# One block from QKV to gate/up, with buffers at fixed places and each stage's first inputs prepared in the stage ahead

## The chip, the cores and the metric

The kernel runs on one core of one Trainium2 chip. The metric is the device time of one execution in microseconds (us). TensorE (PE in the profile) multiplies matrices; VectorE (DVE), ScalarE (ACT) and GpSimd (POOL) work element by element; SyncE (SP) issues most of the transfers. Engines run their own streams of instructions in order and wait for one another by semaphores.

## The reference

An AdaLN transformer layer in float32: 2048 tokens, width 1024, 32 query heads and 8 key/value heads of 32 columns, no mask, and a feed-forward part of width 2752 whose activations are truncated to 8-bit integers.

```python
mod = (_silu(L0_c) @ L0_wmod).reshape(L0_c.shape[0], 6, 1, -1)
sa, ca, ga, sb, cb, gb = (mod[:, 0], mod[:, 1], mod[:, 2], mod[:, 3], mod[:, 4], mod[:, 5])
ga = (2 * (ga >= 0) - 1) * jnp.maximum(jnp.abs(ga), 0.25)      # gb likewise
h = _layernorm(x, axis=-1) * (1 + ca) + sa
x = x + ga * _L0_attn_ref(h, L0_attn_Wq, L0_attn_Wk, L0_attn_Wv, L0_attn_Wo, L0_attn_bo)
h = _layernorm(x, axis=-1) * (1 + cb) + sb
x = x + gb * _L0_ffn_ref(h, L0_ffn_w_gate, L0_ffn_w_up, L0_ffn_w_down)
# attention: softmax(q k^T / sqrt(32)) v per head, then y @ Wo.T + bo
# ffn: trunc(clip(silu(xf Wg^T) * (xf Wu^T) * 128)) as int8, @ Wd^T, trunc(clip(* 128))
```

## The kernel before

Five stage functions follow one another, each with its own buffers and its own `nc.Block`. At the end of a block all engines meet at a barrier, and then go to the code of the next block. Float32 operands are split in a high and a low part, and each product is three matmuls (`TERMS`): high by high, high by low, low by high.

- `stage_modulation_and_qkv`: four blocks of 512 tokens. In the last one PE also multiplies the scores for the row maxima of attention's unit 0 (`first_turn`). SP stores the two rows of maxima into `qs0` (line 232). The stage ends when every store of q, k and v has landed (the waits at the end of POOL's and ACT's code).
- `stage_attention`: 32 units, one for each of 8 key/value heads and 4 blocks of 512 queries, with 16 key tiles (k = 0 to 15) each. For a key tile PE makes four transposed score tiles (line 954), ACT takes their exponential (853), and at every even k PE multiplies two earlier key tiles by v (`by_v`, 965). Between them PE multiplies the scores of the next units (`turn`, 940), of which DVE takes maxima (872). POOL adds pairs of exponentials (797), DMAs add such pairs (806), and PE sums three of these over the keys (`denominators`, 980). In unit 0 turns start at k = 2; in unit 31 there are none, and most of unit 30's are done early. After unit 31 PE multiplies the last denominators, DVE takes eight reciprocals (898) and the product (902), SP stores y. The output weights `wo_raw` are loaded early, unsplit.
- `stage_out_projection`: 16 tiles of 128 tokens, in a loop for the middle 12. It first loads y of tiles 0 and 1 (1098), splits y (1147 on ACT, 1177 on DVE) and the weights (1151, 1182), and prepares the gate on DVE (`gate_of`). For tile t PE runs `project(t + 1)`, 48 matmuls (1237), then eight transposes of the normalised tile t (1250); ACT scales them (1165); DVE adds bias, gate and x, and normalises (1207 to 1217), splits y of tile t + 2 and splits the second layer input of tile t - 1 (1198, 1200). All low parts go to memory (`h2lo_dram`) by POOL and come back by SP.
- `stage_gate_up`: 22 tiles of 128 hidden columns, each by four blocks of 512 tokens (n). For each n PE runs 24 matmuls for gate and 24 for up (1446). The next weights are split by ACT (1373) and DVE (1398) within a tile.
- `stage_down`: its own block, before and after the change.

Every engine issues in the order of its code; there is no planner.

Of the kernel before, what the change touches and what calls it, by code (L numbers as in the profile page):

```python
# [11 lines left out]
P = 128  # L12
# [26 lines left out]
def overlay(nc, stack, *views):  # L39

    out = []
    for i, (name, shape, dt) in enumerate(views):
        one = nc.sbuf_tensor(name, shape, dt)
        if i + 1 < len(views):
            with one as tensor:
                out.append(tensor)
        else:
            out.append(stack.enter_context(one))
    return out
# [35 lines left out]
def stage_modulation_and_qkv(nc, ctx, c, wmod, x, wq_t, wk_t, wv_t, mod_dram, q_dram, k_dram, v_dram, modT, ident,  # L85
                             hT0_hi, kq0):
# [14 lines left out]
    with ExitStack() as st:  # L101
        def sb(name, shape, dt=F32):
            return st.enter_context(nc.sbuf_tensor("qkv_" + name, shape, dt))

        def pb(name, width=NB):
            return st.enter_context(nc.psum_tensor("qkv_" + name, [P, width], F32))

        def sem(name):
            return st.enter_context(nc.semaphore("qkv_" + name))

        w = [sb(f"wqkv_{n}", [P, MW, FT, P], F32R) for n in ("hi", "lo")]
        wraws = sb("wqkv_raw", [P, 2, FT, P])
        wraw = [wraws[:, i] for i in range(2)]
        hT_1 = [overlay(nc, st, (f"qkv_wmod_{n}", [P, 2, GW], F32), (f"qkv_hT1_{n}", [P, FT, NB], F32R))
                for n in ("hi", "lo")]
        hT = [[hT0_hi, sb("hT0_lo", [P, FT, NB], F32R)], [i[1] for i in hT_1]]
        xt = [sb(f"x_tile{i}", [P, D]) for i in range(2)]
        stats = [sb(f"ln_stats{i}", [P, 12]) for i in range(2)]
        mv = [sb(f"ln_mv{i}", [P, 2]) for i in range(2)]
        s = [sb(f"ln_s{i}", [P, 8]) for i in range(2)]  # L120
        aff = [sb(f"h_affine{i}", [P, FT, P]) for i in range(2)]
        qko = [[sb(f"qk_out{i}_{n}", [P, NB], F32R) for n in ("hi", "lo")] for i in range(2)]
        vo = [sb(f"v_out{i}", [P, VW]) for i in range(2)]
        ccol, cwork = sb("c_col", [P, FT]), sb("c_work", [P, 3, FT])
        ones, crep = sb("ones_32", [P, 32]), sb("silu_c_rep", [P, FT, 32])
        rows = sb("mod_rows", [P, NB])
        wmod_own = sb("wmod", [P, GW])
# [6 lines left out]
        cmax0, rmax0 = sb("chunk_max0", [P, NTURN]), sb("row_max0", [P, GH * BT])  # L134
        mT0 = [sb(f"max_T0_{n}", [GH * BT, P], F32R) for n in ("hi", "lo")]
        tr = pb("h_T", 2 * NB)
        qkp = [pb(f"qk_acc{i}") for i in range(QKB)]
        vp = [pb(f"v_acc{i}") for i in range(2)]
        modp = pb("mod_acc")

# [28 lines left out]
        block = st.enter_context(nc.Block(no_gpsimd_drain=True))  # L169
# [25 lines left out]
        def _(sp):  # L195
# [77 lines left out]
        def _(act):  # L273
# [50 lines left out]
            for i in range(2):  # L324
                act.wait_ge(v_stored[i], 16 * TT // 2)

# [215 lines left out]


def stage_attention(nc, ctx, q_dram, k_dram, v_dram, y_dram, den_dram, kq0, ident, wo_t, wo_raw, wo_loaded):
# [35 lines left out]
    with ExitStack() as st:  # L580
        def sb(name, shape, dt=F32):
            return st.enter_context(nc.sbuf_tensor("att_" + name, shape, dt))
# [50 lines left out]
        def bank(u, c, i):  # L633

            return (order(u, c) + i) % NST
# [1186 lines left out]
```

## Time and profile before

| | us |
|---|---|
| median of three runs | 3582.47 (3580.29 to 3582.48) |
| the profiled execution | 3583.01 |
| its span, first to last instruction | 3581.2 |
| PE busy | 3462.8 (97%) |
| DVE busy | 2218.3 (62%) |
| POOL busy | 1602.9 (45%) |
| ACT busy | 1600.1 (45%) |

The span is what the trace covers; the execution's own time is 1.8 us longer. The stages hold about these stretches of the span: QKV 0 to 375, attention 383.6 to 2052, output projection 2055 to 2262, gate/up 2271 to 3238, down 3241 to 3581. "PEclk" in a row of the windows view is the TensorE clock that was granted: 1.00 is 2.4 GHz, 0.50 is 1.2 GHz.

### The profile page before, as it was taken

The numbers are of one execution on the slowest core, as the hardware profiler recorded it, in microseconds if no ns is written. First come the engines' busy times: TensorE is split into PE (matmuls) and PEld (weight loads), VectorE is DVE, ScalarE is ACT, GpSimd is POOL, SyncE is SP. The second block draws the span as 40 slices with busy tenths as digits, with TensorE's granted clock in tenths as the row PEclk, the third lists the DMA queues.
The fourth block names the chain that finished last, engine by engine and source line by source line (L and its number), as shares of the span: only waits on it lengthen the run. The fifth ranks groups of instructions, "written<-read, shape, count | busy, mean of one in ns | idle before, by whom it ended". The sixth has DMA issues, their size and how long they took to land. (4 is left out here: it accounts for less than half of the span.)

```text
span 3581.2 us, 46156 instructions
## 1 busy us (share of the span) xinstructions
PE 3462.8 (97%) x17196; PEld 2314.1 (65%) x17196; DVE 2218.3 (62%) x3730; ACT 1600.1 (45%) x2990; POOL 1602.9 (45%) x701
## 2 busy tenths in 40 slices
PE   6999899999999999999999699799999999998998
PEld 4778455555555555555555288688888888887786
DVE  5545677777777777777777088444444444442727
ACT  3210466666666666666666433222222222213544
POOL 1111488989989899899889700000000000000010
PEclk8999899999999999999999899899999999999999
DMA  6662555656555555556554445611111111113212
GB/s 228 206 189 82 131 119 107 123 109 123 112 115 113 112 121 111 116 112 122 110 107 95 91 166 173 182 29 29 29 30 29 29 29 29 30 41 118 94 64 86
DMA packets 196090, 361.96 MB, mean 101 GB/s; under 512 B 41744, under 2 KB 122896, under 8 KB 175696
## 3 DMA queue, kind: packets, MB, share of 16 engines
q0 software_dynamic: 37120, 202.92, 24.9%
q1 hardware_dynamic: 156496, 154.69, 15.7%
q8 instruction: 104, 1.70, 0.2%
q10 hardware_dynamic: 2304, 2.10, 0.2%
q14 instruction: 66, 0.54, 0.0%
HBM read 162.13 MB, written 62.78 MB: 63 GB/s over the span
## 5 line engine op out<-in xcount | busy, mean ns | idle before, releaser
L872 DVE TENSOR_REDUCE att_chunk_max<-att_scores 128x1 f32<-128x512 f32 x1984 | 1212.9, 682 | 352.1 <-PE att_scores L940 352.1
L853 ACT ACTIVATE att_exp<-att_scores_T 128x512 f32<-128x512 f32 x2048 | 1049.5, 621 | 449.9 <-PE att_scores_T L954 441.8
L797 POOL TENSOR_TENSOR att_exp_pair<-att_exp 128x2048 f32<-128x2048 f32 x256 | 1199.7, 4737 | 62.8 <-ACT att_exp L853 62.3
L965 PE MATMUL att_y_acc<-att_exp,att_v_head 128*32 128x512 f32 x4096 | 499.0, 605 | 0.0
L1327 POOL DMA_DIRECT2D inter_scratch<-gu_inter x84 | 45.2, 538 | 882.6 <-DVE gu_inter L1270 882.6
L940 PE MATMUL att_scores<-att_kq,att_q_stack 96*128 96x512 f32 x768 | 327.3, 430 | 3.8 <-DMA att_q_stack<-q_scratch 2.4
L940 PE MATMUL att_scores<-att_k_stack,att_q_stack 96*128 96x512 f32 x768 | 325.0, 426 | 0.3
L954 PE MATMUL att_scores_T<-att_q_stack,att_k_stack 98*128 98x512 f32 x768 | 299.3, 412 | 2.4 <-ACT att_exp L853 2.3
L954 PE MATMUL att_scores_T<-att_q_stack,att_kq 98*128 98x512 f32 x768 | 296.4, 405 | 0.7 <-ACT att_exp L853 0.7
L1381 ACT ACTIVATE gu_magnitude<-gu_value 128x512 f32<-128x512 f32 x88 | 55.7, 633 | 516.7 <-DVE gu_value L1412 516.7
L1411 DVE TENSOR_TENSOR gu_rounded<-gu_up_acc,gu_rounded 128x512 f32<-128x512 f32 x88 | 60.9, 692 | 323.7 <-PE gu_up_acc L1446 323.7
L965 PEld LDWEIGHTS att_y_acc<-att_exp,att_v_head 128*32 128x32 f32 x4096 | 107.4, 109 | 216.6 <-ACT att_exp L853 116.7
L940 PEld LDWEIGHTS att_scores<-att_kq,att_q_stack 96*128 96x128 f32 x768 | 144.8, 189 | 149.3 <-DVE att_chunk_max L872 86.8
L1446 PE MATMUL gu_gate_acc<-h_hi,shared_split 128*128 128x512 f32 x704 | 225.7, 392 | 11.7 <-DVE shared_split L1398 11.7
L940 PEld LDWEIGHTS att_scores<-att_k_stack,att_q_stack 96*128 96x128 f32 x768 | 144.3, 188 | 139.4 <-DVE att_chunk_max L872 77.2
L1446 PE MATMUL gu_up_acc<-h_hi,shared_split 128*128 128x512 f32 x704 | 223.9, 389 | 0.0
L954 PEld LDWEIGHTS att_scores_T<-att_q_stack,att_k_stack 98*128 98x128 f32 x768 | 144.3, 189 | 74.5 <-ACT att_exp L853 49.6
L954 PEld LDWEIGHTS att_scores_T<-att_q_stack,att_kq 98*128 98x128 f32 x768 | 145.1, 189 | 55.5 <-ACT att_exp L853 32.6
L1237 PE MATMUL wo_wo_acc<-wo_wo_hi,shared_split 128*128 128x512 f32 x512 | 164.2, 397 | 13.7 <-DVE shared_split L1177 13.5
L806 POOL DMA_DIRECT2D att_exp_pair<-att_exp_pair x128 | 111.7, 873 | 127.5 <-DMA att_exp_pair<-att_exp_pair 93.2
L1446 PEld LDWEIGHTS gu_gate_acc<-h_hi,shared_split 128*128 128x128 f32 x704 | 133.2, 189 | 40.0 <-issue 12.1
L1446 PEld LDWEIGHTS gu_up_acc<-h_hi,shared_split 128*128 128x128 f32 x704 | 132.2, 188 | 27.5
(222 smaller groups left out, 6059.8 us busy)
## 6 DMA issues: line engine op xcount, KB each, us to landing
att_exp_pair<-att_exp_pair POOLq DMA_DIRECT2D x128, 1024.0 KB, 7.2
att_q_stack<-q_scratch SPq DMA_DIRECT2D x72, 256.0 KB, 5.8
shared_raw<-in_wd_t POOLq DMA_DIRECT2D x34, 256.0 KB, 3.3
qkv_x_tile<-in_x SPq DMA_DIRECT2D x16, 512.0 KB, 4.7
q_scratch<-qkv_qk_out_hi POOLq DMA_DIRECT2D x32, 256.0 KB, 3.1
q_scratch<-qkv_qk_out_lo POOLq DMA_DIRECT2D x32, 256.0 KB, 4.2
qkv_wqkv_raw<-in_wmod POOLq DMA_DIRECT2D x8, 1024.0 KB, 7.3
qkv_wmod<-in_wmod POOLq DMA_DIRECT2D x8, 1024.0 KB, 8.2
```

The source lines that it names most:

```text
L797: nc.gpsimd.tensor_tensor(ps[PAIR_SLOT[j]][:], pr[2 * j % NP][:], pr[(2 * j + 1) % NP][:], ALU.add).then_inc(pair_done, 1)
L806: pool.dma_start(ps[into][:], ps[other][:], accum_op=ALU.add).then_inc(dma_sum[i], 16)
L853: nc.scalar.activation(pr[k % NP][:, h * NB:(h + 1) * NB], stp[bank(u, c, GH * k + h)][:], ACT.Exp, scale=INV_SQRT_DH).then_inc(exp_done, 1)
L872: nc.vector.reduce_max(cmax[c % 2][:, q:q + 1], turn_buffer(u, c, q)[:], AX.X).then_inc(sm_done, steps_done(u, q))
L940: nc.tensor.matmul(turn_buffer(u, c, q)[:], qs[c % 4][0:SR, h, qt * P:(qt + 1) * P], ks[c // QB % 2][0:SR, kc * NB:(kc + 1) * NB], start=T ...
L954: nc.tensor.matmul(stp[bank(u, c, i)][:], ks[c // QB % 2][0:SR + 2, k * P:(k + 1) * P], qs[c % 4][0:SR + 2, h, :], start=True, stop=True). ...
L965: ins = nc.tensor.matmul(yp[h * DH:(h + 1) * DH, :], vg[c // QB % 2][:, k, :], pr[k % NP][:, h * NB:(h + 1) * NB], start=(k == 0), stop=(k ...
L1237: ins = nc.tensor.matmul(acc[j][:, half * NB:(half + 1) * NB], ysp[j][a][:, k, :], w[z][:, k, half * NB:(half + 1) * NB], start=(k == 0 an ...
L1327: eng.dma_start(inter_dram[i, 0:LASTI if last else P, n * NB:(n + 1) * NB], out[n % 2][rows, :]).then_inc(last_stored if last else out_sto ...
L1381: nc.scalar.activation(mag[:], val[:], ACT.Abs)
L1411: ln.link(nc.vector.tensor_tensor(rnd[:], up[n % 2][:], rnd[:], ALU.mult))
L1446: ins = nc.tensor.matmul(bank[n % 2][:], w[j][a][:, m * HALF_W + k * P:m * HALF_W + (k + 1) * P], h2[z], start=(k == 0 and q == 0), stop=( ...
```

## The change

QKV, attention, output projection and gate/up share one `nc.Block`. The three barriers between them are gone, and semaphores that the stages hand on take their place. All buffers get fixed offsets (`place`, `bank`), so that what one stage fills does not lie on what the one ahead still uses.

- QKV to attention: SP loads q of units 1 and 2 and v of the first head within QKV, ahead of its wait for unit 0's maxima; ACT runs one Exp at the end of QKV. PE's attention code waits for `v_evac` at its start and for `qk_evac` at k = 2.
- Attention: the output weights are loaded in unit 0 as 16 transfers. Their high parts are copied by ACT in units 30 and 31 (eight copies of 128x512 each, two after h = 2 of k = 2, 4, 8, 10), their low parts by DVE after unit 30's work, with the reciprocal of unit 30 in between. y of tiles 0 and 1 is loaded and split within unit 31. The last denominators, division and store of y go into the output projection's tiles 0 and 1.
- Output projection: unrolled, no loop. The gate and bias loads go from POOL's queue to SP's, after unit 31's scores. Low parts of tiles 0 to 3 stay on chip (`h2_lo0`). The first gate/up weights are loaded at t = 14 and split by ACT and DVE around t = 14 and 15. The last tile's transposes, scaling, split and store of x go into gate/up's first tile.
- Gate/up: tiles 0 and 1 are taken out of the loop. For n = 0 the low part is read as four pieces of 128 columns, because `h2_lo0` is laid out by tile.
- Down keeps its block, now `nc.Block()` without `no_gpsimd_drain`.

```diff
@@ stage_modulation_and_qkv, SP: ahead of the wait for mT0_done
+            for u in (1, 2):
+                for r, n in enumerate((0, 0, 1)):
+                    sp.dma_start(qs[u][r * DH:(r + 1) * DH].bitcast(F32),
+                                 q_dram[n].rearrange("(h d) t -> d h t", d=DH)[:, 0:GH, u * NB:(u + 1) * NB].bitcast(F32)
+                                 ).then_inc(q_loaded[u], 16)
+            for i in range(2):
+                sp.wait_ge(v_stored[i], 16 * TT // 2)
+            sp.dma_start(vg[0][:], v_dram[:, 0:DH].rearrange("(k p) d -> p k d", p=P)).then_inc(v_loaded, 16)
...
@@ stage_attention, SP
+                if u == NU - 1:
+                    sp.wait_ge(y_stored, 16 + 16 * (NU - 2))
+                    sp.wait_ge(*first_y_room)
+                    sp.wait_ge(pv_done, NP + u * KT + KT // 2 + 2)
+                    for t in range(2):
+                        wo.load_y(sp, t)
...
@@ stage_attention, ACT
+                        if u >= NU - 2 and k in WO_HI_AT and h == GH - 2:
+                            for i in (2 * WO_HI_AT.index(k), 2 * WO_HI_AT.index(k) + 1):
+                                act.wait_ge(wo.loaded, 32 * FT)
+                                nc.scalar.copy(wo.hi[:, u - NU + 2, i, :], wo.raw[:, u - NU + 2, i, :]).then_inc(wo.hi_done, 1)
+                        if u == NU - 1 and k == TSTEP and h == GH - 2:
+                            act.wait_ge(*first_y_room)
+                            act.wait_ge(pv_done, NP + u * KT + KT // 2 + 2)
+                            wo.hi_of_y(act, 0)
...
@@ stage_attention, DVE
-            units(v, unit)
-            last_unit(NU - 1, NU - 1)
+            for u in range(NU - 1):
+                unit(u, u % BODY, u // QB)
+            wo_lo(0, range(FT))
+            wo_lo(1, range(FT // 2))
+            recip(NU - 2)
+            wo_lo(1, range(FT // 2, FT))
+            for t in range(2):
+                wo.lo_of_y(v, t)
...
@@ stage_out_projection, ACT
+            for t in range(TT):
+                if t == TT - 1:
+                    act.wait_ge(acc_done, TT)
+                    gu.weights_hi(act, 0, 0, 1)
                 act.wait_ge(var_done, t + 1)
...
+                if t == TT - 2:
+                    act.wait_ge(acc_done, TT - 1)
+                    act.wait_ge(gu.loaded[0], 32)
+                    gu.weights_hi(act, 0, 0, 0)
+                if t < TT - 1:
+                    affine(act, t)
...
@@ stage_out_projection, DVE: ahead of tile 15, and after tile 0
+                if t == TT - 1:
+                    for m in range(2):
+                        gu.weights_lo(v, 0, 0, m)
...
+                if t == 0:
+                    att["division"](v)
+                else:
+                    split(v, t - 1)
...
@@ stage_out_projection, PE
+            project(0)
+            for t in range(TT - 1):
+                if t:
+                    pe.wait_ge(x1_done, t)
+                project(t + 1)
+                if t == 0:
+                    att["denominators"](pe)
+                transposes(pe, t)
...
@@ stage_gate_up, PE
+                    pe.wait_ge(out_proj["h_split"], BT * (n + 1))
+                    if n:
+                        pe.wait_ge(h_loaded[n], 16 * BT)
...
+                            low = h2_lo[n][:, k, :] if n else h2_lo0[:, :, k, :]
...
+                    if is_first(i) and n == 0:
+                        out_proj["transposes"](pe)
...
@@ build
+        with nc.Block(no_gpsimd_drain=True) as block:
+            qkv = stage_modulation_and_qkv(nc, ctx, block, c, wmod, x, wq_t, wk_t, wv_t, mod_dram, q_dram, k_dram, v_dram,
+                                           modT, ident, kq0, qs, vg, q_loaded, v_loaded)
...
+        with nc.Block() as block:
+            stage_down(nc, ctx, block, wd_t, mod_dram, x1_dram, inter_dram, out, shared[0], down_loaded)
```

New functions that it calls are `OutInputs` (`load_y`, `hi_of_y`, `lo_of_y`: one transfer, one ACT copy and one DVE subtraction for a tile of y) and `GateUpWeights` (`weights_hi`, `weights_lo`: the same for one half of a tile's weights).

## Rows read from the trace of the kernel before

**Rows 1.** The page, busy time of each engine and its share of the span.
```profile
PE 3462.8 (97%) x17196; PEld 2314.1 (65%) x17196; DVE 2218.3 (62%) x3730; ACT 1600.1 (45%) x2990; POOL 1602.9 (45%) x701
```
**Rows 2.** Windows: length, busy us (instructions) of each engine, PEclk, DMA share, GB/s.
```profile
385.00:390.00 5.00, 3.26 (x7) 1.73 (x6) 0.00 (x0) 3.90 (x8) 1.51 (x1) 0.50 0.98 200
...
1985.00:2029.00 44.00, 42.37 (x190) 13.71 (x189) 0.26 (x1) 27.92 (x56) 39.37 (x13) 0.89 0.50 103
```
**Rows 3.** Timeline of PE, QKV to attention: start, length, work [idle before <-releaser].
```profile
383.55 4.71 PE L954 MATMUL att_scores_T<-att_kq 98*128 98x512 f32 x9 [8.65 <-DVE att_ones L921]
390.62 1.22 PE L940 MATMUL att_scores<-att_kq,att_q_stack 96*128 96x512 f32 x2 [2.36 <-DMA att_q_stack<-q_scratch]
...
393.90 3.64 PE L965 MATMUL att_y_acc<-att_exp,att_v_head 128*32 128x512 f32 x16
...
404.18 1.92 PE L965 MATMUL att_y_acc<-att_exp,att_v_head 128*32 128x512 f32 x16
```
**Rows 4.** Timeline of SP's queue, the store of unit 0's maxima.
```profile
373.74 0.57 SPq L232 DMA_DIRECT2D att_kq<-qkv_max_T_lo  x1
```
**Rows 5.** Line 232, time of its two transfers from issue to landing.
```profile
DMA to landing us min/median/max: 2.4/2.6/2.8
```
**Rows 6.** Timeline of PE, attention to output projection.
```profile
2030.14 1.90 PE L980 MATMUL att_den_acc<-att_exp_pair,att_ones 128*32 128x512 f32 x16
2045.91 1.94 PE L980 MATMUL att_den_acc<-att_exp_pair,att_ones 128*32 128x512 f32 x8 [13.87 <-DMA att_exp_pair<-att_exp_pair]
2061.33 0.79 PE L1237 MATMUL wo_wo_acc<-wo_wo_hi,shared_split 128*128 128x512 f32 x1 [13.48 <-DVE shared_split L1177]
```
**Rows 7.** Timeline of ACT in unit 31.
```profile
2014.17 4.03 ACT L853 ACTIVATE att_exp<-att_scores_T 128x512 f32<-128x512 f32 x8 [1.39 <-PE att_scores_T L954]
```
**Rows 8.** Timeline of POOL, its last adds.
```profile
2029.63 8.97 POOL L797 TENSOR_TENSOR att_exp_pair<-att_exp 128x2048 f32<-128x2048 f32 x2
```
**Rows 9.** Line 797, ns min/median/max, 500 to 1900 us.
```profile
L797 POOL TENSOR_TENSOR att_exp_pair<-att_exp x221: 4555/4862/4922, 499.8 to 1899.1; 128x2048 f32<-128x2048 f32 x111
```
**Rows 10.** Line 797, ns min/median/max, 1975 to 2040 us.
```profile
L797 POOL TENSOR_TENSOR att_exp_pair<-att_exp x10: 4493/4710/4882, 1979.2 to 2034.1; 128x2048 f32<-128x2048 f32 x10
```
**Rows 11.** Timeline of DVE, last division and first tile of the output projection.
```profile
2047.91 3.45 DVE L898 RECIPROCAL att_den_acc<-att_den_acc 128x64 f32<-128x64 f32 x8 [39.97 <-PE att_den_acc L980]
2051.40 0.69 DVE L902 TENSOR_TENSOR att_y_out<-att_y_raw,att_den_acc 128x512 f32<-128x512 f32 x1
...
2075.84 1.23 DVE L1207 TENSOR_TENSOR wo_gated<-wo_wo_acc,wo_bo_rows 128x1024 f32<-128x1024 f32 x1 [0.90 <-PE wo_wo_acc L1237]
...
2082.90 0.81 DVE L1217 TENSOR_SCALAR wo_x_norm<-wo_x_tile,wo_ln_mv,wo_ln_s 128x1024 f32<-128x1024 f32 x1
2083.63 1.22 DVE L1177 TENSOR_TENSOR shared_split<-shared_raw,shared_split 128x1024 fp32r<-128x1024 f32 x1
```
**Rows 12.** Timeline of PE, last tiles of the output projection to gate/up.
```profile
2239.71 1.04 PE L1250 MATMUL wo_h_T<-ident,wo_x_norm 128*128 128x128 f32 x8
2240.51 0.47 PE L1237 MATMUL wo_wo_acc<-wo_wo_hi,shared_split 128*128 128x512 f32 x1
...
2251.52 1.03 PE L1250 MATMUL wo_h_T<-ident,wo_x_norm 128*128 128x128 f32 x8
2259.64 1.97 PE L1250 MATMUL wo_h_T<-ident,wo_x_norm 128*128 128x128 f32 x8 [7.09 <-DVE wo_x_norm L1217]
2273.33 0.77 PE L1446 MATMUL gu_gate_acc<-h_hi,shared_split 128*128 128x512 f32 x1 [11.72 <-DVE shared_split L1398]
```
**Rows 13.** Timeline of ACT at the same place.
```profile
2252.59 2.89 ACT L1165 ACTIVATE wo_h_affine<-wo_h_T,mod_cols 128x128 f32<-128x128 f32 x8 [6.70 <-PE wo_h_T L1250]
...
2270.78 1.99 ACT L1373 CAST shared_split<-shared_raw 128x1024 fp32r<-128x1024 f32 x2 [6.08 <-PEq L1040]
```
**Rows 14.** Timeline of PE, gate/up's second block of tokens, its second matmul.
```profile
2286.91 0.39 PE L1446 MATMUL gu_gate_acc<-gu_h_lo,shared_split 128*128 128x512 f32 x1
```
**Rows 15.** Windows, line 505 alone: length, busy us (matmuls), then busy us (weight loads).
```profile
115.10:125.00 9.90, 9.90 (x83) 9.90 (x83) 1.00 0.84 270
```

More of the change, by code:

```diff
@@ L36, with place, bank, in_order @@
 SHARED = max(6 * HALF_W, IT * QW)
[L39 to L48, printed above, removed]
+R0 = 704
+R1, R2, R3, R4, R5, BIG = (R0 + n * 1024 for n in (16, 32, 40, 48, 56, 64))
+TAIL = BIG + 140 * 1024
+PR, PS = BIG, BIG + 64 * 1024
+WO_AT, DEN_AT_ROW = BIG + 104 * 1024, BIG + 136 * 1024
+def place(nc, offset, name, shape, dt):
+    if offset == 0:
+        with nc.sbuf_tensor(name, shape, dt) as tensor:
+            return tensor
+    with nc.sbuf_tensor("below_" + name, [P, offset // 4], F32):
+        with nc.sbuf_tensor(name, shape, dt) as tensor:
+            return tensor
+def bank(nc, nth, name, width=NB):
+    if nth == 0:
+        with nc.psum_tensor(name, [P, width], F32) as tensor:
+            return tensor
+    with nc.psum_tensor("below_" + name, [P, nth * NB], F32):
+        with nc.psum_tensor(name, [P, width], F32) as tensor:
+            return tensor
+def in_order(first, *sizes):
+    out = [first]
+    for n in sizes:
+        out.append(out[-1] + n)
     return out
@@ L914, in unit @@
                             recip(u - 1)
-                    if not ahead and k == RECIP_AT:
-                        recip(u - 1)
                     if k == TSTEP - 2 and not beyond(u, 1):
@@ L1068, in stage_out_projection @@
-        y_hi, y_split, acc_done, x1_done, x1_stored = (
-            sem("y_hi"), sem("y_split"), sem("acc_done"), sem("x1_done"), sem("x1_stored"))
+            return ctx.enter_context(nc.semaphore("wo_" + name))
+        BT = NB // P
+        xt = [sb(f"x1_tile{i}", [P, D], F32, R2 + i * 4 * D) for i in range(2)]
+        gate, bias = sb("gate_a", [P, D], F32, R3), sb("bo_rows", [P, D], F32, R3 + 4 * D)
+        offs = in_order(BIG + 4 * SHARED, 4 * D, 4 * D, 4 * D, 4 * D)
+        work, xn, aff = sb("gated", [P, D], F32, offs[0]), sb("x1_norm", [P, D], F32, offs[1]), sb("h2_affine", [P, FT, P], F32, offs[2])
@@ new lines, in affine, with split @@
+        def affine(act, t):
+            act.wait_ge(tr_done, t + 1)
+            act.wait_ge(h_split, t)
+            for f in range(FT):
+                ins = nc.scalar.activation(aff[:, f, :], tr[f * P // NB][:, f * P % NB:f * P % NB + P], ACT.Identity,
+                                           scale=modT[:, 32 + f:33 + f], bias=modT[:, 24 + f:25 + f])
+            ins.then_inc(aff_done, 1)
+        def split(v, t):
+            v.wait_ge(aff_done, t + 1)
+            if t == BT - 1:
+                v.wait_ge(*att["y_stored"])
+            if t > BT:
+                v.wait_ge(lo_stored, 16 * (t - BT))
+            for half in range(2):
+                fs = slice(half * FT // 2, (half + 1) * FT // 2)
+                hi = h2_hi[half][:, :, t * P:(t + 1) * P]
+                low = h2_lo0[:, t, fs] if t < BT else lo[t % 2][:, fs]
+                nc.vector.tensor_copy(hi, aff[:, fs]).then_inc(h_hi, 1)
+                v.wait_ge(h_hi, t * 2 + (half + 1))
+                ins = nc.vector.tensor_tensor(low, aff[:, fs], hi.bitcast(F32), ALU.subtract)
+            ins.then_inc(h_split, 1)
@@ L1128, in _ @@
[L1128 to L1129 removed]
+                    load_x(t + 2)
+                if t == 1:
+                    att["store_y"](sp)
+                    sp.wait_ge(*att["y_stored"])
         @block.gpsimd
         def _(pool):
[L1133 to L1135 removed]
@@ L1307, in stage_gate_up @@
+        h_loaded = [None] + [sem(f"h2lo_loaded{b}") for b in range(1, QB)]
         g_acc, u_acc, sig_done, val_done, parts_done, out_done, out_stored = (
```

637 lines of the change are left out of this document (311 added, 326 removed).

## The prediction

> **What bounds the kernel now.** I read the page's busy shares first. PE is busy 97% of the span and the next engine 62% [rows 1], so time can be gained only where PE stands still or runs at its lower clock. The chain of waits gives nothing on the change: it follows PE back through the down stage alone. I therefore went through PE's timeline at each change of stage, then through the other engines' timelines at the same places.
>
> From QKV to attention PE stands still 8.65 us, then 2.36 us for unit 1's q [rows 3]. From attention to the projection it stands still 13.87 us for the last sum by DMA and 13.48 us for the first y [rows 6]. From the projection to gate/up it stands still 7.09 and 11.72 us [rows 12]. That is 57.2 us in six gaps. After a gap PE also runs at the 1.2 GHz level: the clock is 0.50 in the window after the first [rows 2], and `by_v` takes 3.64 us there against 1.92 later [rows 3]. The gap at down is outside this change.
>
> **A: QKV to attention.** The last QKV matmul ends at 374.9 (383.55 - 8.65) [rows 3]. What unit 0 still needs is its row of maxima: issued at 373.74 [rows 4], landed 2.4 to 2.8 us later [rows 5], so about 376.4; with some 0.4 us for SP to pass its semaphores on, PE starts at 376.8 in place of 383.55. That gives 6.75 us. Of the new waits at PE's start, `v_evac` belongs to values multiplied 60 us earlier, and behind it stands all of attention, so only the maxima count. The wait for `qk_evac` at k = 2 has PE's turns and `by_v` behind it; k = 2 comes about 4.7 us after the start (the length of the first run of scores [rows 3]), when DVE has long split the last tile. DVE's fill of a constant (under 2 us) fits before that as well. The 2.36 us for q go too, since those six loads and that of v are issued some 50 us earlier. On SP they stand behind unit 0's own q and k, so they delay no first turn; the wait for v's stores stands ahead of SP's wait for the maxima, and v is finished by then. A = 9.1 us.
>
> What is late next is ACT: during k = 0 and 1 PE goes at the pace of the exponentials and may again run at the lower clock. The row of that stretch has PE busy 3.26 of 5 us at 0.50 [rows 2], but a long gap stands before it. In unit 31 there are only short waits for ACT, and the clock still averages 0.89 over 44 us [rows 2]. I take the low clock at first, so nothing more is gained on the first `by_v`. The other end is 3.64 - 1.92 = 1.7 us more [rows 3]. The 16 weight loads on SP (8 before) stand ahead of unit 1's maxima store, which is due a whole unit later; no cost.
>
> The Trainium skill ("TensorE: Matmul & The Clock Gate", Loop structure matters more than you think) says that waiting for a copy out of PSUM does not break PE's warmth, only a long wait for a DMA does. By it the new start would stay at 2.4 GHz and A would be 10.8 us. The unit 31 row speaks against it, so it does not change my term.
>
> **B: attention to projection.** `by_v` of unit 31 ends at 2030.1, where the denominators start now [rows 6]. PE goes straight to `project(0)`. ACT has two copies more at each of four places in unit 31, 0.5 to 0.6 us each (half of a copy of 1024 columns, 1.0 us, and a little for the start) [rows 13], about 1.2 us together. They stand just where ACT waits 1.39 us for PE after h = 2 [rows 7], so they hide; in unit 30, where the turns lengthen each pair of key tiles, the wait is longer. If that cover were gone, PE would lose up to 16 x 0.6 = 9.6 us over both units. y of tile 0 is loaded after POOL's fifth pair of unit 31, about 2016 (two adds and two smaller jobs ahead of 2029.6 [rows 8]), and is copied (1.0 us) [rows 13] in the same kind of hole at k = 14.
>
> `project` is 11.0 us (2240.51 to 2251.52) and eight transposes 0.8 us (2239.71 to 2240.51) [rows 12]. Before, `project(0)` ended at about 2075.8, when DVE took it up [rows 11]; new it ends at 2030.1 + 11.0 = 2041.1: 34.7 us earlier. `project(1)` ends at 2052.1. There the denominators come: 1.90 us for two thirds [rows 6], so 2.9 us, to 2055.0. Their last input comes now at 2045.9 [rows 6], so it is not waited for. DVE then takes the reciprocals and product, 3.45 + 0.69 [rows 11], to 2059.2, and only then tile 1, whose chain to the normalised tile is 7.9 us (2075.84 to 2083.7) [rows 11]: 2067.1, plus 1.2 us for y of tile 3 (line 1177) [rows 11], 2068.3. PE would be ready for the transposes of tile 1 at 2066.8 and for `project(3)` at 2067.6, so it loses about 0.8 us. DVE's load a tile stays just under PE's 11.8, so the loss is not repeated. The store of y and its landing hold SP until about 2070; y of tile 4 is needed about 2078. The gate and bias loads, moved to SP, are needed by 2041 and are issued about 2030; if they land at 2039, `gate_of` ends 2.5 us late, and DVE still reaches the division before the denominators. B = 34.7 - 2.9 - 0.8 = 31.0 us. Without the 2.9 us as new work this is the two gaps, the 3.8 us of denominators and 3.7 us of low clock in the first tile.
>
> One cost has no row. DVE now does 16 subtractions with both inputs on chip, and two of y, while POOL adds pairs almost without pause. Before, DVE's work beside POOL was maxima from PSUM. If neither disturbs the other, the cost is zero: POOL's add has a median of 4.86 us beside a busy DVE and 4.71 with DVE idle [rows 9, 10], so reading PSUM costs it little. At the other end each excludes the other for an instruction: DVE gets about one subtraction in between two adds of 4.7 us, so 12 of them take until about 2020 (they start at 1974), the reciprocal of unit 30 and thus SP's load of y follow, and the split of y comes after POOL's last add. That add ends at 2038.6 now [rows 8] and some 4 us later with DVE's pieces between, so `project(0)` starts at about 2043: 13 us. I take 2 us, near the zero that these rows favour.
>
> The Trainium skill ("SBUF — State Buffer", Who interferes with whom) says that a DVE instruction with two SBUF inputs and a GpSimd instruction that reads SBUF lock each other out. No row of before has that pair, so it can't be checked; by the rule the sum loses 11 us of the 58 below. It is a rival.
>
> **C: projection to gate/up.** Let E be 2251.52, when the transposes of tile 14 start [rows 12]. Before, the second block of tokens starts one matmul (0.23) ahead of 2286.91 [rows 14]: E + 35.2. New: transposes to E + 0.8, gate's 24 matmuls (half a `project`, 5.5) to E + 6.3. Up needs its weights: ACT scales tile 14 until E + 4.0 [rows 13], copies for 1.0 us [rows 13], DVE subtracts for 1.2 (1024 columns, as for y) [rows 11]: E + 6.2, just in time. Up ends at E + 11.8. DVE starts tile 15 at E + 6.2 (before: E + 0.2) and has it normalised at E + 14.1, so PE waits 2.3 us, transposes, and starts the second block at E + 15.0. C = 35.2 - 15.0 = 20.2 us. Gate's own weights are loaded from E - 14 on and split at E - 2; ACT's wait for that load has the scaling of tile 14 behind it. If they came 8 us late, C would lose 6. Sigmoid comes with its table load after the last square root, and the last tile's split is due only at the fourth block, at about E + 37; these hide. The low parts loaded back are three blocks instead of four. The peeled tiles issue the same work.
>
> The pieces of 128 columns in gate/up's n = 0 are 22 x 16 = 352 matmuls. Line 505 already reads its moving operand in two such pieces: 83 matmuls of 256 columns in 9.90 us, 0.119 each [rows 15], the same for a column as 0.23 for 512. I cost them at zero; the upper bound is double their 0.227, 80 us. Fixed places alone change no instruction: zero, and a stage of 1650 us bounds it by no row, so I allow 2 us either way. Down's `nc.Block()` may add under 1 us at the end, where POOL is idle.
>
> **The sum.** 9.1 + 31.0 - 2 + 20.2 = 58.3 us. From the profiled execution's 3583.0 that is 3524.7; the median lies 0.5 us below that execution: 3524.
>
> **Rivals.**
> - Ports: DVE and POOL shut each other out in unit 31. For: they do overlap. Against: nothing in these rows shows it. Loss 13 in place of 2: 3535.
> - The barrier's waits live on: one start still waits for a store, a load or a copy. The likeliest is A (maxima landing and the lower clock both later, giving 2 us) or C's weights late (6 us less): 3531. The change then does only part of what it says. Against: each of these inputs has its landing in the rows above.
> - Slower: the 128-column pieces halve PE's rate in those 352 matmuls, 80 us: 3604. It decides from 58.3 / 352 = 0.166 us each. Against: line 505's pace.
> - Better: clock kept, no cost at ports: 3524 - 1.7 - 2 = 3520, inside the forecast.
>
> **Chances.** Forecast 0.55, ports 0.24, waits that live on 0.14, pieces 0.04, and 0.03 for a loss without a name that eats the gain. The range goes from 3514 (6 us past the better case, as copies or clock may give more) to 3541 (ports and late weights together). 0.2%, 7 us, is about what a measurement can tell here: faster by more 0.94, within 0.02, slower 0.04.
>
> **What would show it.** Right: PE gaps of about 2 us at the first place, under 2 at the second, about 2.3 before the last transposes; the first out-projection matmul at about 2023 (2030.1 - 9.1 + 2); denominators after `project(1)`. Wrong in B: DVE's subtractions in unit 31 with starts tied to the ends of POOL's adds, or waits of ACT longer than its copies. Wrong in A: the first score after 377. Wrong at the pieces: starts of those matmuls more than 0.23 us apart. A sum of gaps gone below 45 us would make the prediction wrong.

## The result: 3555.0 us, half of the gain that was forecast

| | before | changed |
|---|---|---|
| median, us | 3581.85 | 3555.02 |
| lowest to highest, 4 runs each | 3580.29 to 3582.48 | 3551.06 to 3556.60 |
| ratio, 95% interval | | 0.9924 [0.9907, 0.9941] |
| profiled execution, us (its span) | 3583.0 (3581.2) | 3555.3 (3553.4) |

The change makes the kernel 26.8 us faster. The forecast was 58 us, to 3524, with a range of 3514 to 3541; the measured time lies outside it.

**Where the gain came.** Read at fixed points of PE's timeline: the first denominators of the attention start 3.8 us earlier (the two rows below, before and after). The transposes of tile 14 start 21.7 us earlier [rows 12], and gate/up's second token block 27.4 us earlier [rows 14]. From there to the end nothing changed. So A gave 3.8 us (forecast 9.1), B 17.9 (29.0) and C 5.7 (20.2). These are readings of one execution each. In the traces of experiments 1, 4, 5, 6 and 7, whose code is the same up to the first denominators, these start at 445.3 to 448.5, so A is 2.5 to 5.7 us.

```profile
450.99 1.04 PE L980 MATMUL att_den_acc<-att_exp_pair,att_ones 128*32 128x512 f32 x8
```
```profile
447.21 1.04 PE L744 MATMUL att_den_acc<-att_exp_pair,att_ones 128*32 128x512 f32 x8
```

The page after, against [rows 1]. DVE is busy 56 us longer with eight instructions more:

```profile
PE 3458.6 (97%) x17196; PEld 2311.9 (65%) x17196; DVE 2274.3 (64%) x3738; ACT 1589.2 (45%) x2990; POOL 1604.0 (45%) x695
```

**QKV to attention**, PE's timeline, then ACT's, then POOL's (start, length, engine, line, work, [idle before <-releaser]); against [rows 3]:

```profile
375.72 0.97 PE L1034 MATMUL att_scores_T<-att_kq 98*128 98x512 f32 x3 [1.55 <-SPq L806]
384.50 3.32 PE L1034 MATMUL att_scores_T<-att_kq 98*128 98x512 f32 x6 [7.81 <-ACT att_exp L922]
...
390.73 3.08 PE L1045 MATMUL att_y_acc<-att_exp,att_v_head 128*32 128x512 f32 x16
```
```profile
383.85 4.60 ACT L922 ACTIVATE att_exp<-att_scores_T 128x512 f32<-128x512 f32 x9 [64.01 <-POOLq L898]
```
```profile
376.45 0.54 POOL L283 DMA_DIRECT2D q_scratch<-qkv_qk_out_lo  x1
```

PE's scores start at 375.7, even ahead of the forecast 376.8. Then PE stops after three of them, for 7.81 us, because ACT makes no exponential. The releaser of ACT is not an engine's work but line 898 in POOL's queue: `sem_inc(pair_done, NP // 2)`, the starting value that says "the eight exponential buffers are free". It needs nothing, but it stands in POOL's queue behind the end of POOL's QKV code, a wait for the last stores of q and k. The last of them was issued at 376.45, and the transfers of that line from 372 to 378 took up to 7.0 us to land:

```profile
DMA to landing us min/median/max: 3.2/4.5/7.0
```

**Attention to projection**, DVE's timeline, then ACT's and PE's; against [rows 6, 11]:

```profile
1970.06 45.19 DVE L977 TENSOR_TENSOR wo_lo<-wo_raw,wo_hi 128x512 fp32r<-128x512 f32 x12
2015.17 0.24 DVE L972 RECIPROCAL att_rden_spread<-att_den_spread 128x16 f32<-128x16 f32 x1
2015.33 16.59 DVE L977 TENSOR_TENSOR wo_lo<-wo_raw,wo_hi 128x512 fp32r<-128x512 f32 x4
```
```profile
2027.66 1.04 ACT L1129 CAST shared_split<-shared_raw 128x1024 fp32r<-128x1024 f32 x1 [6.27 <-DMA shared_raw<-y_scratch]
```
```profile
2029.25 1.28 PE L1034 MATMUL att_scores_T<-att_q_stack,att_k_stack 98*128 98x512 f32 x2 [6.04 <-ACT att_exp L922]
2030.47 3.64 PE L1045 MATMUL att_y_acc<-att_exp,att_v_head 128*32 128x512 f32 x16
2037.42 0.80 PE L1314 MATMUL wo_acc<-wo_hi,shared_split 128*128 128x512 f32 x1 [3.32 <-DVE shared_split L1133]
```

The two gaps of 13.9 and 13.5 us are gone, two smaller ones came. DVE's 16 subtractions last 61.8 us. The line's summary gives least, median and most in ns:

```profile
L977 DVE TENSOR_TENSOR wo_lo<-wo_raw,wo_hi x16: 678/4891/10383, 1970.1 to 2026.9; 128x512 fp32r<-128x512 f32 x16
```

The median is one addition of POOL (4.86 us [rows 9]) and the longest is two of them back to back. One subtraction of DVE and the addition of POOL beside it:

```profile
1976.45 5.06 DVE L977 TENSOR_TENSOR wo_lo<-wo_raw,wo_hi 128x512 fp32r<-128x512 f32 x1
```
```profile
1975.94 5.03 POOL L866 TENSOR_TENSOR att_exp_pair<-att_exp 128x2048 f32<-128x2048 f32 x1
```

It ends at 1981.51, 0.54 us after the addition (1980.97), and every long subtraction of this trace ends so, 0.54 to 0.56 us after one of POOL's instructions. The reciprocal of unit 30 stands behind 12 subtractions, SP's load of y behind the reciprocal, and ACT's copy of y stands in front of the last five exponentials. So PE loses 6.04 us inside the attention and 3.32 us after it. How the loss divides changes from one execution to the next: in experiment 2, with the same code here, PE stops once for 16.14 us inside the attention and not after it, but the time from the first denominators to the projection's first matmul is nearly the same, 1591.8 us there and 1590.2 here.

**Projection to gate/up**, PE's timeline, then DVE's and ACT's; against [rows 12, 13]:

```profile
2229.86 1.04 PE L1196 MATMUL wo_h_T<-ident,wo_x_norm 128*128 128x128 f32 x8
2245.26 0.76 PE L1536 MATMUL gu_gate_acc<-h_hi,shared_split 128*128 128x512 f32 x1 [14.36 <-issue]
...
2259.55 0.40 PE L1536 MATMUL gu_gate_acc<-gu_h_lo,shared_split 128*128 128x512 f32 x1
```
```profile
2245.13 0.69 DVE L1219 TENSOR_TENSOR wo_h_lo<-wo_h_affine,h_hi 128x512 fp32r<-128x512 f32 x1
```
```profile
2245.24 1.28 ACT L1468 ACT_TABLE_LOAD   x1 [3.43 <-DVEq L1513]
```

PE stands still 14.36 us and the profile names only "issue": no semaphore event of a compute instruction or a transfer explains it. ACT's row at the same moment names the cause. Line 1513 in DVE's queue is `v.sem_inc(val_done, 2)`, again a starting value. It stands behind all of DVE's projection code, whose last instruction started at 2245.13.

### The profile page after: what moved, and what is told of

Read it like the earlier page. It is cut to its first block and busy times, and to the rows that moved or that the text cites. A ratio compares the mean times of both kernels' runs of the same rounds, so it can differ in the third digit from the quotient of the medians.

```text
span 3553.4 us, 45601 instructions
## 1 busy us (share of the span) xinstructions
PE 3458.6 (97%) x17196; PEld 2311.9 (65%) x17196; DVE 2274.3 (64%) x3738; ACT 1589.2 (45%) x2990; POOL 1604.0 (45%) x695
## 5 line engine op out<-in xcount | busy, mean ns | idle before, releaser
L1314 PE MATMUL wo_acc<-wo_hi,shared_split 128*128 128x512 f32 x512 | 163.2, 396 | 3.4 <-DVE shared_split L1133 3.3
L1536 PEld LDWEIGHTS gu_gate_acc<-h_hi,shared_split 128*128 128x128 f32 x704 | 133.3, 189 | 42.4 <-issue 14.6
L1468 ACT ACTIVATE gu_sigmoid<-gu_gate_acc 128x512 f32<-128x512 f32 x88 | 52.7, 599 | 235.5 <-PE gu_gate_acc L1536 235.5
```

Source lines behind the costliest of these rows:

```text
L1314: ins = nc.tensor.matmul(acc[t % 2][:, half * NB:(half + 1) * NB], wo.ysp[t % 2][a][:, k, :], (wo.hi, wo.lo)[z][:, half, k, :], start=(k = ...
L1536: ins = nc.tensor.matmul(dst, gu.w[j][m][a][:, k * P:(k + 1) * P], h2[z], start=(k == 0 and q == 0), stop=(k == FT - 1 and q == 2))
```

## Experiments

Times below are medians; each ratio is to the kernel before, run on the same chip. The intervals are about 6 us to either side, so a smaller difference from the changed kernel rests on its trace and not on the ratio. Unless a diff says otherwise all else is as in the changed kernel.

### 1. No wait for gate/up's starting value

```diff
                 for n in range(QB):
-                    pe.wait_ge(val_done, n + 1 + i * QB)
+                    if not (is_first(i) and n < 2):
+                        pe.wait_ge(val_done, n + 1 + i * QB)
...
-                    act.wait_ge(val_done, n + 2 + i * QB)
+                    if not (is_first(i) and n == 0):
+                        act.wait_ge(val_done, n + 2 + i * QB)
```

> Edit: TensorE does not wait on the value counter for the first two token blocks of gate/up tile 0, nor ScalarE for the first; the counter's starting value is given by VectorE from its gate/up code, which stands behind its whole output projection. Theory (credit): in the changed kernel TensorE stands 14.4 us ahead of its first gate matmul (to 2245.3) for that starting value alone. Without the wait the gate's 24 matmuls start within 2 us of tile 14's transposes (2229.9), the granted clock stays at full speed there, and tile 15's transposes and the second token block follow VectorE's last normalisation, at about 2244 to 2247 where it was 2259.2: 3555 becomes 3541 to 3544. Rival (the gap is TensorE's own: loading of instructions, or the weights' split): the gap stays above 10 us and the time stays at 3553 to 3556.

Measured: 3540.7 us (3538.6 to 3542.5), ratio 0.9889 [0.9872, 0.9906]. PE's timeline:

```profile
2227.68 1.04 PE L1196 MATMUL wo_h_T<-ident,wo_x_norm 128*128 128x128 f32 x8
2228.47 0.47 PE L1538 MATMUL gu_gate_acc<-h_hi,shared_split 128*128 128x512 f32 x1
...
2241.57 1.09 PE L1196 MATMUL wo_h_T<-ident,wo_x_norm 128*128 128x128 f32 x8 [1.91 <-DVE wo_x_norm L1295]
...
2242.73 0.39 PE L1538 MATMUL gu_gate_acc<-gu_h_lo,shared_split 128*128 128x512 f32 x1
```

The gap is gone, 14.3 us with it. The second block starts 0.23 us ahead of 2242.73, 14.8 us after tile 14's transposes; the forecast's working had 15.0, and 1.9 us of wait where it had 2.3. The instruction stream and the weights hold nothing up.

### 2. No wait for the exponentials' starting value

```diff
-                            act.wait_ge(pair_done, k // 2 + 1 + u * PAIRS)
+                            if not (is_first(u) and k < NP):
+                                act.wait_ge(pair_done, k // 2 + 1 + u * PAIRS)
```

> Edit: ScalarE does not wait on GpSimd's pair counter for the first 8 key blocks of the first unit (their exponential buffers are free; the counter's starting value is given by GpSimd behind its wait for the last stores of QKV). Theory (credit through GpSimd): the first exponential starts at 377 to 378 where it was 383.9, so the first product with V is at 384 to 385 instead of 390.7, and the time is 5 to 7 us lower, 3548 to 3550. Rival (the exponentials or the scores are held by SP's loads or by the table load as well): the first product with V stays after 388, and the time changes by less than 3 us.

Measured: 3547.2 us (3546.0 to 3548.5), ratio 0.9907 [0.9890, 0.9923], 7.8 us less than the changed kernel, slightly more than expected. ACT's timeline, then PE's:

```profile
376.63 4.51 ACT L923 ACTIVATE att_exp<-att_scores_T 128x512 f32<-128x512 f32 x9 [56.17 <-PE att_scores_T L1035]
```
```profile
377.28 3.01 PE L1035 MATMUL att_scores_T<-att_kq 98*128 98x512 f32 x6 [0.22 <-ACT att_exp L923]
...
383.17 2.13 PE L1046 MATMUL att_y_acc<-att_exp,att_v_head 128*32 128x512 f32 x16
```

The first denominators start at 438.69, 12.3 us earlier than before. That is 3.2 us more than A's 9.1; experiment 8 has the same code here and gives 10.0, because its first score came at 378.33 where this one's came at 376.10. From the first score to the first denominators both take 62.6 us, against 67.4 before: 4.8 us less, where the forecast counted only the 2.36 us for unit 1's q. The clock is part of it. Windows of 378 to 392 us (length, busy us of PE, PEld, DVE, ACT and POOL, granted clock, DMA share, GB/s), the changed kernel and then this one:

```profile
378.00:392.00 14.00, 7.50 (x21) 4.27 (x25) 3.26 (x6) 5.79 (x11) 4.02 (x1) 0.55 1.01 343
```
```profile
378.00:392.00 14.00, 13.43 (x52) 6.59 (x55) 9.78 (x18) 8.78 (x17) 6.66 (x2) 0.88 0.99 337
```

With only short waits for ACT the clock averages 0.88 and the first `by_v` takes 2.13 us; behind the 7.8 us gap it is 0.55 and 3.08 us. The Trainium skill ("TensorE: Matmul & The Clock Gate", Loop structure matters more than you think), whose rule on copies out of PSUM the forecast set aside for unit 31's row, comes closer here: its A was 10.8 us, and 2.13 us is nearer to `by_v` at full clock (1.92 [rows 3]) than to the 3.64 that the forecast took.

### 3. Wo's loads a unit later

```diff
-                if is_first(u):
+                if u == 1:
                     for half in range(2):
                         for k in range(FT):
                             sp.dma_start(wo.raw[:, half, k, :], ...)
```

> Edit: the 16 loads of Wo are issued in unit 1 of the attention instead of unit 0; the waits stay as they are. It tells how much of the late start of the exponentials is the landing of the last stores of QKV behind those loads. Theory (crowding): the stores land in about 3.3 us as in the kernel before (issued at 376.4, so at 379.7), and the first exponential starts at 380 where it was 383.9: 3551 to 3552. Rival (the stores are late for another cause, such as the three loads of q in unit 0): the first exponential stays at 383 to 384 and the time at 3555.

Measured: 3563.0 us (3555.1 to 3566.5), ratio 0.9946 [0.9929, 0.9962]: 8 us slower than the changed kernel in the median, but one of the four runs, 3555.1, was not slower at all. At the place that was asked about, the first exponential came at 382.65, neither 380 nor 384. The landing of the stores (line 255 before, then line 283 here):

```profile
DMA to landing us min/median/max: 2.7/3.0/3.3
```
```profile
DMA to landing us min/median/max: 2.7/3.9/5.4
```

Its longest is 5.4 us, where the changed kernel had 7.0. That doesn't show that the sixteen loads are part of the crowding: in experiment 1, where they stand in unit 0 as in the changed kernel, the longest is 5.2 us and the first exponential comes at 382.75. Why the stores land later than before (3.3) stays open. The loss came in unit 1. SP's timeline, then PE's:

```profile
443.16 13.49 SPq L821 DMA_DIRECT2D wo_raw<-in_wo_t  x16
...
466.67 7.38 SPq L792 DMA_DIRECT2D den_scratch<-att_den_rows  x1
```
```profile
482.50 0.80 PE L1020 MATMUL att_scores<-att_kq,att_q_stack 96*128 96x512 f32 x1 [7.23 <-DVE att_chunk_max L952]
```

One issue in SP's queue after those loads lasted 7.38 us; no other of that line takes over 0.6 us in this trace. The loads are the only edit, but why this one issue took so long is not shown. Unit 0's denominators come late by it. DVE waits for them with its reciprocal (7.3 us), the maxima queued behind it are not taken, and PE stops for 7.23 us. In unit 0 the same loads cost nothing of the kind, since no trip of denominators follows them there.

### 4. Wo's low parts in 4 instructions instead of 16

```diff
-                for k in ks:
-                    v.wait_ge(wo.hi_done, half * FT + k + 1)
-                    nc.vector.tensor_tensor(wo.lo[:, half, k, :], ...).then_inc(wo.lo_done, 1)
+                for k in ks[::4]:
+                    v.wait_ge(wo.hi_done, half * FT + k + 4)
+                    nc.vector.tensor_tensor(wo.lo[:, half, k:k + 4, :], ...).then_inc(wo.lo_done, 4)
```

> Edit: the 16 subtractions of 512 columns that make Wo's low parts are 4 of 2048 columns. Theory (VectorE and GpSimd exclude each other, and a subtraction gets in only between two additions of GpSimd): each of the 4 lasts one wait for an addition, up to 4.9 us, and its own 2.4 us, so 4 last under 30 us in place of 61; the reciprocal of unit 30's denominators runs before 2008 instead of 2015.2, ScalarE no longer holds the last exponentials for y (6.3 us), and the output projection starts at 2028 to 2032 instead of 2037.4: 3546 to 3550. Rival (a shared rate: both engines slow down in proportion to what they move): 4 of 2048 columns last as long as 16 of 512, about 15 us each, the last reciprocal is at 2015 or later, and the time is 3554 to 3557.

Measured: 3545.0 us (3543.3 to 3546.1), ratio 0.9899 [0.9882, 0.9915], 10.0 us less. DVE's timeline, then POOL's and PE's:

```profile
1970.20 9.63 DVE L977 TENSOR_TENSOR wo_lo<-wo_raw,wo_hi 128x2048 fp32r<-128x2048 f32 x2
1989.67 11.56 DVE L977 TENSOR_TENSOR wo_lo<-wo_raw,wo_hi 128x2048 fp32r<-128x2048 f32 x1 [9.84 <-ACT wo_hi L931]
2001.36 0.25 DVE L972 RECIPROCAL att_rden_spread<-att_den_spread 128x16 f32<-128x16 f32 x1
2010.52 2.29 DVE L977 TENSOR_TENSOR wo_lo<-wo_raw,wo_hi 128x2048 fp32r<-128x2048 f32 x1 [8.90 <-ACT wo_hi L931]
```
```profile
2011.04 6.19 POOL L866 TENSOR_TENSOR att_exp_pair<-att_exp 128x2048 f32<-128x2048 f32 x1
```
```profile
2026.55 0.50 PE L1314 MATMUL wo_acc<-wo_hi,shared_split 128*128 128x512 f32 x1
```

The same columns take 23.5 us in 4 instructions and 61.8 in 16. The last one, which starts before POOL's next addition, lasts 2.29 us, and the addition that starts inside it lasts 6.19 us instead of 4.86. The exclusion works both ways. The projection starts 10.9 us earlier than in the changed kernel and somewhat ahead of what was expected.

### 5. The same work in 32 instructions

```diff
-                    nc.vector.tensor_tensor(wo.lo[:, half, k, :], ...).then_inc(wo.lo_done, 1)
+                    for cs in (slice(0, NB // 2), slice(NB // 2, NB)):
+                        ins = nc.vector.tensor_tensor(wo.lo[:, half, k, cs], ...)
+                    ins.then_inc(wo.lo_done, 1)
```

> Edit: the 16 subtractions of 512 columns are 32 of 256, the same work in twice the instructions. Theory (VectorE gets in between two additions of GpSimd, one or so instruction each time, whatever its size): their mean stays near 3.8 us each while GpSimd adds, so only some 14 to 17 of 32 are done when its last addition ends at about 2036, the reciprocal (behind 24 of them) runs at 2036 or later, y is late, and the output projection starts at 2050 or later: 3566 or more. Rival (a shared rate): 32 of half the size last half as long each, 1.9 us, nothing moves: 3553 to 3557.

Measured: 3558.5 us (3558.2 to 3558.9), ratio 0.9936 [0.9919, 0.9952], 3.5 us more than the changed kernel, which the intervals don't tell apart; the expectation of 3566 or more missed, and so, by little, did the rival's 3553 to 3557. DVE's windows (length, busy us and instructions of `wo_lo`, clock, DMA) and POOL's timeline:

```profile
2008.00:2012.00 4.00, 4.00 (x1) 1.00 1.04 211
2012.00:2016.00 4.00, 4.00 (x12) 1.00 0.42 84
```
```profile
2007.36 4.86 POOL L866 TENSOR_TENSOR att_exp_pair<-att_exp 128x2048 f32<-128x2048 f32 x1
2014.25 0.87 POOL L875 DMA_DIRECT2D att_exp_pair<-att_exp_pair  x1 [2.03 <-DMA att_exp_pair<-att_exp_pair]
```

While POOL adds, one instruction of half the size is as stuck as one of full size. When POOL waits 2.03 us for a transfer, DVE does about a dozen in 4 us. About half of these run beside POOL's next addition, from 2014.86, and this time it is the addition that is held: it lasts 6.74 us. "One for each addition" left out POOL's pauses. The reciprocal, behind 24 of the 32, came at 2017.1. A rate shared between the engines, the rival, gives neither row of DVE.

### 6. The reciprocal behind 8 subtractions instead of 12

```diff
-            wo_lo(1, range(FT // 2))
             recip(NU - 2)
-            wo_lo(1, range(FT // 2, FT))
+            wo_lo(1, range(FT))
```

> Edit: in the last unit VectorE takes the reciprocal of unit 30's denominators after 8 of the 16 subtractions instead of after 12; sizes unchanged. It separates the two costs of the slow subtractions. Theory (both count): the reciprocal runs at 2005 to 2008 instead of 2015.2, ScalarE no longer waits 6.3 us for y, TensorE ends the attention at about 2027 to 2028 instead of 2034.1, but Wo's and y's low parts are still subtracted one for each of GpSimd's additions and end near 2033 to 2036, so the output projection starts there (2037.4 before): 3550 to 3554. Rival (only the late reciprocal counts): the output projection starts by 2029, and the time is 3545 to 3547.

Measured: 3555.8 us (3547.8 to 3560.1), ratio 0.9921 [0.9904, 0.9937]: no gain, and a wide spread. In the profiled execution, the longest of the four:

```profile
1971.98 43.48 DVE L977 TENSOR_TENSOR wo_lo<-wo_raw,wo_hi 128x512 fp32r<-128x512 f32 x8
```

The reciprocal follows at 2015.38, where it was at 2015.17 in the changed kernel. Eight took as long as twelve had, because in the changed kernel the ninth to the twelfth had cost almost nothing. They ran in one pause of POOL between two additions:

```profile
2012.76 2.49 DVE L977 TENSOR_TENSOR wo_lo<-wo_raw,wo_hi 128x512 fp32r<-128x512 f32 x4
```

So the edit could bring the reciprocal at most 2.5 us forward, and here the eight also started 1.9 us later. A subtraction's cost depends on where POOL stands, and a count of them is no measure of time. The experiment was meant to separate the late reciprocal from the late low parts, and it does not.

### 7. Short additions on POOL in the last unit

```diff
-                nc.gpsimd.tensor_tensor(ps[PAIR_SLOT[j]][:], ...)
+                cs = slice(0, GH * NB // 4 if u == NU - 1 else GH * NB)
+                nc.gpsimd.tensor_tensor(ps[PAIR_SLOT[j]][:, cs], ...)
...
-                nc.gpsimd.tensor_tensor(ps[4][:], ps[4][:], ps[1][:], ALU.add).then_inc(quad_done, 1)
+                cs = slice(0, GH * NB // 4 if u == NU - 1 else GH * NB)
+                nc.gpsimd.tensor_tensor(ps[4][:, cs], ps[4][:, cs], ps[1][:, cs], ALU.add).then_inc(quad_done, 1)
```

> Left out: in the last unit GpSimd's eight pair sums and its sum of four add only the first 512 of their 2048 columns, so the last block's denominators are not whole; its waits and its DMA sums are unchanged, and so are all of VectorE's 16 subtractions of 512 columns. Theory (VectorE's slow subtractions wait for GpSimd's additions): with additions of 1.2 us in place of 4.8 the 16 subtractions last 0.7 to 1.9 us each, under 30 us in all (61.8 in the changed kernel), the ninth to the sixteenth end soon after ScalarE's last high parts (2010), the reciprocal of unit 30 runs by 2007, and the output projection starts at 2026 to 2028: 3543 to 3546. Rival (they are slow from the DMA traffic or from ScalarE's reads of the same buffers, both unchanged): they stay at a median near 4.9 us, and the output projection starts at 2035 or later.

Measured: 3537.6 us (2 runs), ratio 0.9875 [0.9846, 0.9903]. DVE's work on `wo_lo` is unedited:

```profile
L979 DVE TENSOR_TENSOR wo_lo<-wo_raw,wo_hi x16: 676/684/5061, 1969.6 to 2006.3; 128x512 fp32r<-128x512 f32 x16
```
```profile
2021.01 0.50 PE L1316 MATMUL wo_acc<-wo_hi,shared_split 128*128 128x512 f32 x1
```

The median falls from 4.89 to 0.68 us. The long ones left stand beside unit 30's whole additions, but for one of 3.83 us beside two short ones back to back. POOL's additions are the cause. The projection also starts 5 us earlier than expected, and the clock is part of it. Windows of 2000 to 2015 us, the changed kernel, this one, and experiment 1, whose additions are whole:

```profile
2000.00:2015.00 15.00, 14.56 (x54) 4.38 (x54) 15.00 (x7) 10.96 (x23) 12.64 (x6) 0.77 0.54 109
```
```profile
2000.00:2015.00 15.00, 14.34 (x64) 5.08 (x56) 2.76 (x5) 12.81 (x27) 7.09 (x7) 1.00 0.98 210
```
```profile
2000.00:2015.00 15.00, 14.34 (x70) 5.10 (x70) 15.00 (x9) 12.80 (x26) 12.66 (x5) 1.00 0.49 98
```

PE is busy about as long in all three and gets fewer matmuls done at 0.77. The traces of experiments 4 and 8 have the dip too (0.77), those of 5 and 6 don't (1.00). Experiment 1 has the changed kernel's code up to here and stays at 1.00, so the shorter additions are not shown to have removed the dip; its cause stays open. In the changed kernel it seems to cost nothing: experiment 1, without it, takes as long from the first denominators to the projection (1590.5 us against 1590.2), since it waits longer for y.

### 8. The three edits together

Edits 1, 2 and 4.

> Edit: the changed kernel with the three edits together: no wait for the two starting values (first exponentials; first gate/up blocks) and Wo's low parts in 4 instructions. Theory (three separate hidden waits are all that is missing): the gains add, 14.3 + 7.8 + 10.0 = 32.1 us off the changed kernel's 3555.0: 3521 to 3525, and the sum on record (3524) is met. Rival (they share a part, or what is late next takes some of it back): 3527 or more; the place to look is VectorE's wait for the rows of bo ahead of the output projection's first tile, which appeared when the projection started earlier.

Measured: 3523.8 us (3522.8 to 3525.2), ratio 0.9839 [0.9823, 0.9855]. The gains add, and this is the fastest version: 31 us under the changed kernel. PE's timeline at the fixed points:

```profile
440.97 1.04 PE L744 MATMUL att_den_acc<-att_exp_pair,att_ones 128*32 128x512 f32 x8
...
2020.56 0.50 PE L1315 MATMUL wo_acc<-wo_hi,shared_split 128*128 128x512 f32 x1
...
2213.17 1.04 PE L1197 MATMUL wo_h_T<-ident,wo_x_norm 128*128 128x128 f32 x8
...
2228.22 0.39 PE L1539 MATMUL gu_gate_acc<-gu_h_lo,shared_split 128*128 128x512 f32 x1
```

A is 10.0 us (450.99 - 440.97), A and B together 38.4 (2251.52 - 2213.17 [rows 12]), so B 28.3, and C 20.3 (2286.91 - 2228.22 = 58.7, less 38.4) [rows 14]. The recorded terms were 9.1, 29.0 and 20.2. DVE's wait of 8.9 us for the rows of bo, named by the rival, is there, and PE loses 1.3 us to it at the first transposes. PE also waits 1.5 us for the last sum by DMA, which the forecast expected to be early.

## Why the prediction was wrong

**The sum is that of a kernel without three waits; the changed kernel has them.** Each of the three takes back what its experiment returned: 14.3 + 7.8 + 10.0 = 32.1 us, and 3555.0 less that is 3522.9. What is left after them came to within 1 us of each term in experiment 8's trace, but part of that is luck. Within A, PE's start gained 5.2 us (383.55 - 378.33) in place of 6.75, and the stretch behind it 4.8 in place of 2.36. Within B, the projection's start gained 30.8 us beyond A (2061.33 - 2020.56 [rows 6], less 10.0) in place of 29.2, and from there to tile 14's transposes 2.4 us were lost (192.6 against 190.2) where the working had 0.2.

**A, "so only the maxima count": failed.** I followed PE's waits at its start and found them early. ACT's were not followed. Its wait for a free exponential buffer has a starting value that POOL gives, and POOL gives it in order, behind a wait for stores. The forecast gave "some 0.4 us for SP to pass its semaphores on"; POOL's queue needed the same reading, and cost 7.8 us. A gave 3.8 us in place of 9.1. The sign "the first score after 377" that I set for a wrong A did not show: the first score came at 375.7 and the next ones 8.8 us later. The low clock at the first `by_v`, which the forecast took as on record (3.64 us), is there behind the gap (3.08), and mostly absent without it (2.13 and, in experiment 8, 2.30).

**B, "I take 2 us, near the zero that these rows favour": failed.** The rows compared reads of PSUM by DVE beside POOL, and they say nothing about two inputs in SBUF. The rival named Ports had the mechanism, its 12 subtractions, the late reciprocal and its size: 13 us to 3535 of its own. Experiment 4 gives 10.9 at the projection's start. Its picture of DVE done by 2020 and the start at 2043 less A became 2015 and 2037.4. One step it did not have: ACT's copy of y stands ahead of five exponentials, so the late y cost 6.04 us inside the attention, and the low clock followed (0.50 in `by_v` at 3.64 us). The rule of the Trainium skill ("SBUF — State Buffer", Who interferes with whom) for two SBUF inputs is borne out: 4.89 us median beside whole additions, 0.68 with short ones, and 0.68 for each that falls in a pause of POOL. ACT's copies did hide, as forecast: behind those of 2001.65 and 2008.74 ACT still waits 2.0 us for PE.

**C, "transposes to E + 0.8, gate's 24 matmuls": failed.** I followed gate's weights, up's weights and the tile's low parts. The counter of freed results I passed over, as its buffers were plainly free. Its starting value came at E + 15.4 (2245.26 - 2229.86), so gate began at 2245.3 with the clock at 0.50, and C was 5.7 us. Experiment 1 restores 20.3.

**The rival "The barrier's waits live on"** had the right kind and too small a size: 3531 at one place, 0.14. It happened at two places, with Ports at a third: A, B and C fell short by 5.3, 11.1 and 14.5 us, which makes 3555. The range ended at 3541, for Ports and late weights together; no case had all three. The pieces of 128 columns and the fixed places cost nothing: from gate/up's second block to the end the span takes 1294.3 us before (3581.2 - 2286.9) and 1293.9 after (3553.4 - 2259.5). Of the signs, "a sum of gaps gone below 45 us" came true: PE's stops at these places still add up to 33.1 us (1.55 + 7.81 + 6.04 + 3.32 + 14.36), so 24.1 of the 57.2 are gone. So did both signs set for B, subtractions tied to the ends of POOL's additions and a wait of ACT (6.27 us) longer than its copies.

## What to carry to other kernels

When a barrier between two stages is removed, list every starting value that a later stage's code gives with `sem_inc`, and ask what stands ahead of it in the queue of the engine that gives it. It waits for that engine's whole earlier stage, and all who wait for it wait too; leave the wait out where it is true from the start, or give the value before the earlier stage (the second was not tried here). A gap that the profile puts down to "issue" can be such a case: look at what the other engines' queues did in that moment. Put DVE's work on two SBUF inputs beside POOL's additions only in few, large instructions, and keep anything urgent out of the queue behind them. The first is what experiment 4 did; the second is argued, since experiment 6 did not get to test it.

## What the hardware showed unexpectedly

- DVE's subtraction of 512 columns lasts 0.68 us in a pause of POOL, 4.8 to 5.9 us beside one whole addition of POOL (changed kernel and experiment 6) and 10.4 beside two back to back. Four times the columns in one instruction takes 2.29 us when not held and 11.56 beside two additions, so there it costs hardly more. POOL's addition is held too, 6.19 for 4.86 us.
- An instruction with one SBUF input was held as well. In experiment 4 the scaling of 1024 columns at line 1342 lasted 1.81 us while POOL's last additions ran, and 0.68 without them in the changed kernel. This fits the Trainium skill ("SBUF — State Buffer", Who interferes with whom), by which `tensor_scalar` can enter a mode that takes both ports and so contend with GpSimd.
- One DMA issue in SP's queue lasted 7.38 us some 10 us after 16 loads of 256 KB had been issued (experiment 3); the others of that line take 0.54 to 0.58 us in the changed kernel.
- The same stores of q took up to 3.3 us to land before the change, 7.0 in the changed kernel's trace, 5.2 in experiment 1's with the same loads, and 5.4 in experiment 3's without Wo's 16 loads.
- The granted clock between 2000 and 2015 us was 0.77 in some traces and 1.00 in others, with the same code up to there in the changed kernel and in experiment 1, and with PE busy 14.3 to 14.6 of the 15 us in both.
